# Moving the second ln_g multiplication, the quantisation of x and the squares within the issue orders of GpSimd, VectorE and ScalarE

## What is computed

```python
x = _layernorm(x + attn(x))                    # 16 heads of 32, every linear with a rank-16 update
x = _layernorm(x + x * scan(ctx * ctx))        # r = decay * r + ctx*ctx along the rows
x = _layernorm(x + ffn(x))

def ffn(x):
    h = silu(bitlinear158(x, w1, b1))          # 512 -> 2048
    h = gelu(h)
    h = layer_norm(h, ln_g, ln_b)              # (h - mean) * rsqrt(var + eps) * ln_g + ln_b
    return bitlinear158(h, w2, b2)             # 2048 -> 512
```

## Time and profile before

| what | value |
| --- | --- |
| median of three executions | 1051.56 us |
| the profiled execution, its own time | 1050.57 us |
| the profiled execution, its span | 1048.7 us |
| mean granted TensorE clock | 0.960 of full speed |
| busy: TensorE, VectorE, ScalarE, GpSimd | 945.9, 907.5, 827.6, 605.9 us |
| distance of one body from the next (565.94 to 623.98, starts of one multiplication by ln_g) | 58.0 us |

### The profile page before, as it was taken

How to read it: one execution, slowest core, us unless ns; L and a number is a source line. 1 busy time by engine, 2 the same in 40 slices (tenths; PEclk the granted TensorE clock), 3 DMA queues, 4 the chain that set the end, 5 groups by cost and what they waited for, 6 DMA issues and landing times.

```text
span 1048.7 us, 23313 instructions
## 1 busy us (share of the span) xinstructions
PE 945.9 (90%) x9260; PEld 650.5 (62%) x9260; DVE 907.5 (87%) x1490; ACT 827.6 (79%) x957; POOL 605.9 (58%) x767
## 2 busy tenths in 40 slices
PE   5998997999999999999999999999999999977515
PEld 3866756676677767676767766676767676644202
DVE  4678878999998999999999989999999999995766
ACT  3646686888979797988879897979888888977684
POOL 2332337474756759485756658494857576572643
PEclk9998998999999999999999999999999999988668
DMA  9432200223122121323131221323131321112213
GB/s 360 154 119 104 73 2 21 74 52 84 22 75 61 48 68 52 84 52 84 48 88 21 60 69 39 83 52 84 52 84 23 93 41 54 44 49 64 52 33 89
DMA packets 106352, 73.67 MB, mean 70 GB/s; under 512 B 91386, under 2 KB 91386, under 8 KB 104451
## 3 DMA queue, kind: packets, MB, share of 16 engines
q1 hardware_dynamic: 105522, 70.34, 24.4%
q10 hardware_dynamic: 720, 1.84, 0.5%
HBM read 41.73 MB, written 8.40 MB: 48 GB/s over the span
## 4 chain that ended last, share of the span: by engine, by line
DVE 34%; PE 28%; ACT 15%; issue 9%; POOL 7%; DMA 7%; SPq 1%; DVEq 0%; ACTq 0%; POOLq 0%
PE bank L1484 11%; PE bank L1345 7%; DVE neg_max L964 6%; DVE h L1095 6%; POOL h L549 5%; DMA xqT<-xq 5%; DVE stats L1021 3%; ACT h L725 3%; ACT junk L735 3%; ACT h L740 3%; PE bank L1485 3%; DVE fz L1100 2%; DVE qk_parts L987 2%; DVE rows L1037 2%; ACT L725 2%
## 5 line engine op out<-in xcount | busy, mean ns | idle before, releaser
L964 DVE TENSOR_REDUCE neg_max<-wave 128x8 f32<-128x2048 f32 x64 | 146.1, 2283 | 19.2 <-PE wave L1370 19.1
L549 POOL TENSOR_TENSOR h<-h,g_tile 128x2048 f32<-128x2048 f32 x30 | 139.4, 4645 | 39.1 <-ACT h L740 39.1
L657 ACT ACTIVATE probs<-wave 128x1024 f32<-128x1024 f32 x128 | 124.4, 1024 | 35.9 <-PE wave L1394 35.7
L1484 PE MATMUL bank<-w,xqT 128*128 128x512 fp8e4 x496 | 130.1, 386 | 23.7 <-DMA xqT<-xq 23.7
L439 POOL TENSOR_SCALAR attn_hi<-attn 128x256 fp32r<-128x256 f32 x64 | 30.2, 473 | 148.6 <-DVE attn L1003 132.9
L695 ACT ACTIVATE rows<-rows,rstd 128x512 f32<-128x512 f32 x96 | 74.3, 807 | 41.7 <-POOL rstd L455 23.8
L719 ACT ACTIVATE h<-bank,qx 128x512 f32<-128x512 f32 x124 | 83.9, 689 | 25.4 <-PE bank L1485 23.2
L1095 DVE TENSOR_TENSOR h<-h,b_tile 128x2048 f32<-128x2048 f32 x32 | 83.9, 2623 | 18.2 <-POOL h L549 18.1
L1484 PEld LDWEIGHTS bank<-w,xqT 128*128 128x128 bf16 x496 | 47.8, 99 | 81.4 <-issue 20.8
L1491 PE MATMUL bank<-w,hqT 128*128 128x512 fp8e4 x416 | 94.3, 380 | 0.2 <-DMA hqT<-h 0.2
L498 POOL TENSOR_TENSOR rows<-rows,bo_tile 128x512 f32<-128x512 f32 x32 | 51.6, 1633 | 71.1 <-DMA rows<-x 71.1
(11 more groups left out here) (184 smaller groups left out, 2841.9 us busy)
## 6 DMA issues: line engine op xcount, KB each, us to landing
ctx_sb<-ctxT SPq DMA_DIRECT2D x16, 512.0 KB, 3.7
rows<-x SPq DMA_DIRECT2D x16, 512.0 KB, 4.0
out<-rows SPq DMA_DIRECT2D x32, 256.0 KB, 2.5
xT_in<-xT SPq DMA_DIRECT2D x15, 512.0 KB, 4.7
h<-w1T SPq DMA_DIRECT2D x4, 1024.0 KB, 14.8
h<-w2T SPq DMA_DIRECT2D x4, 1024.0 KB, 4.9
h<-Wq SPq DMA_DIRECT2D x1, 1024.0 KB, 6.1
h<-Wk SPq DMA_DIRECT2D x1, 1024.0 KB, 9.7
```

Of the source, the lines that this page charges most:

```text
L549: po.tensor_tensor(h_of(b, q)[:, :], h_of(b, q)[:, :], g_tile[:, :], ALU.mult).then_inc(done, 1)
L657: ac.activation(probs[:, kt, :, :], wave[:, :, kt * T:(kt + 1) * T], ACT.Exp, scale=SM_SCALE).then_inc(S["probs_ready"], 1)
L964: dv.tensor_reduce(neg_max[:, :, :], wave[:, :, :].rearrange("p j (t k) -> p j t k", t=NT), axis=AX_X, op=ALU.max, negate=True).then_inc(S ...
L1484: pe.matmul(p[:, :], xqT[:, q, kc, :], w1[:, kc, n * FW:(n + 1) * FW], start=(kc == 0), stop=False)
```

## The change

Three issue orders change. On GpSimd the second half's multiplication by ln_g goes from before `inverse_std2` and `x_rms` to behind them. On ScalarE the squares of the first half go behind the second normalisation, and those of the second half from before `xq_store` to directly before `zq_store`. On VectorE the quantisation of x goes ahead of the second half's addition of ln_b. No instruction is added or removed, and the lead-in, the drain, SP's order and TensorE's order stay as they are.

```diff
@@ GpSimd, body(j)
                 if alive(j, 0):
                     attn_split(j, 1)
-                if alive(j, 2):
-                    g_mul(j - 2, 1)
                 if alive(j, 1):
                     inverse_std2(j - 1)
                     x_rms(j - 1)
+                if alive(j, 2):
+                    g_mul(j - 2, 1)
                 if alive(j, 3):
                     inverse_std3(j - 3, 1)
@@ ScalarE, body(j)
-                if alive(j, 2):
-                    z_square(j - 2, 0)
                 if alive(j, 1):
                     normalise(2, j - 1, 0)
                     normalise(2, j - 1, 1)
+                if alive(j, 2):
+                    z_square(j - 2, 0)
                 if alive(j, 0):
                     shiftT(j, 3)
                 if alive(j, -1):
                     v_store(j + 1, 0)
                 if alive(j, 0):
                     probs_of(j, 3)
-                if alive(j, 2):
-                    z_square(j - 2, 1)
                 if alive(j, 1):
                     xq_store(j - 1)
...
                 if alive(j, 0):
                     ctx_square(j)
                 if alive(j, 2):
+                    z_square(j - 2, 1)
                     zq_store(j - 2, 0)
@@ VectorE, body(j)
                 if alive(j, 0):
                     attn_norm(j, 2)
-                if alive(j, 2):
-                    z_add(j - 2, 1)
                 if alive(j, 1):
                     quantise_x(j - 1)
                 if alive(j, 2):
+                    z_add(j - 2, 1)
                     quantise_z(j - 2, 0)
```

## The result

The change makes the kernel slower: 1106.01 us in the median of four executions (1103.93 to 1109.27) against 1052.07 for the kernel before, run beside it. The ratio is 1.0515, with a 95% interval from 1.0486 to 1.0544. The prediction was 1105.

A forecast was written before the change was run, and what follows sets the result against it. VectorE's order was taken to bound the loop body, through x to TensorE and z to ScalarE. Nine bodies at 4.6 us, three at 3.4 and 2 us for body 15 made 53.6 us, so 1105 us; whole range 1089 to 1114.

The forecast's parts named there:

- What moves on GpSimd: GpSimd's ln_g multiplication starts 0.4 to 0.5 us ahead of VectorE's shift split; ScalarE's second normalisation some 2 us sooner.
- The hold: VectorE's split of the shift, L971, waits for GpSimd's multiplication to end, so VectorE loses 4.04 us.
- What comes back: On VectorE, L1066 in x's quantisation gives back 0.28 us, so the rounding of z ends 3.76 us later.
- z's path: ScalarE's SiLU 0 empties its PSUM bank late, so the fourth feed-forward product on TensorE starts 3.4 us late.
- TensorE's path: TensorE's transposes of the shift start 3.86 us late; absorbing the 0.78 us wait for x leaves 3.1.
- The clock: TensorE's new hole lowers its clock in nine of twelve bodies, costing 1.5 us where it falls, 4.6 us in all.
- The ends: Body 15, outside the twelve bodies, loses 2 us, between 0 and 3.8; body 2 loses nothing.
- Rival 1: The hold on VectorE comes without a fall of TensorE's clock: 43 us lost, 1094.5 us; chance 0.25.
- Rival 3: VectorE's L971 gets in first; the multiplication holds x's quantisation for 1.2 us instead: 4 us lost, 1056; chance 0.07.
- Rival 2: The multiplication never holds VectorE; x lands sooner and the gain, capped by SiLU 0, is 5 us, 1046; chance 0.06.

The follow-up runs named there:

- experiment 3: The changed kernel with the second half's ln_g multiplication one step further back on GpSimd, behind inverse_std3 of the second half: 1067.91 us.
- experiment 6: The changed kernel with the second ln_g multiplication of the bodies cut into four pieces of 512 columns: 1069.22 us.
- 7: The changed kernel with the second ln_g multiplication of the bodies replaced by one memset, so its result differs: 1045.19 us.
- experiment 5: The changed kernel with the first half of v's projection computed twice more on TensorE in bodies 3 to 14, filling its hole: 1091.03 us.
- experiment 4: The kernel before with only x's quantisation moved ahead on VectorE and the second half's squares moved on ScalarE: 1044.05 us.
- experiment 1: The kernel before with only GpSimd's second-half ln_g multiplication moved behind inverse_std2 and x_rms: 1110.8 us.

## Why the prediction was right

- **What moves on GpSimd.** x_rms was to end 3.91 us after the statistics, with the multiplication 3.9 to 4.0 us after them. It started after 3.87 (609.50 to 613.37), 0.53 us ahead of the split where I gave 0.4 to 0.5. ScalarE's second normalisation started 2.42 us after the statistics instead of 4.40, the 2 us sooner that I gave.
- **The hold.** 4.04 us were lost by the sum, and 3.87 were measured (4.04 less 0.17). The multiplication takes 4.54 us here, not 4.64, and starts a little sooner. The Trainium skill's statement in "SBUF — State Buffer", section "Who interferes with whom", that issue order decides and that two SBUF inputs on VectorE meet a read on GpSimd, agrees with experiments 3 (0.17 us when VectorE is first), 6 (one piece each) and 7 (0.17 us beside a memset).
- **What comes back.** The 0.60 us of L1066 fell to 0.17: 0.43, where I had given 0.28. The rounding of z ended 19.72 us after the statistics (609.50 to 629.22) instead of 16.31, 3.41 us later and not 3.76.
- **z's path, 3.4 us a body.** With the clock out of the way (experiment 5) the body is 3.29 us longer, and the fourth part of the feed-forward 3.13 later after the statistics.
- **TensorE's path.** The transposes of the shift were to be 3.86 us late; 8.71 us after the statistics instead of 5.06 is 3.65. Less the 0.78 that is absorbed that leaves 2.9, below the 3.13 of z's path in experiment 5, so without the clock TensorE doesn't decide; with it, it does, as the chain of waits of body 9 shows.
- **The clock.** The hole of 3.44 to 3.81 us was about as long as forecast, and the clock fell behind it. But two numbers were off, in opposite directions. I had it fall in nine of twelve bodies, for a total of 4.6 us each, without a row that gives the count. It fell in all twelve. In nine the body gained 4.2 us on average, in three 5.2. Nine at 4.6 and three at 3.4 are 51.6 us, and the measured sum is 53.6. That a count too low and a price too high came out so near is luck.
- **The ends.** 2 us were given to body 15 and the drain. They took 0.8, and what lies ahead of the twelve bodies, which has nothing to do with the change, another 0.9. So the 1 us between 1105 and 1106 says less than the body times do.
- **The rivals.** Rival 1, the hold without the clock, stood at 1094.5, and experiment 5 put it at 1091. Rival 3, VectorE first, stood at 1056, and experiment 3 gave 1068: the place was right and the price was too low by 1 us a body, mostly because it counted one held instruction of three. Rival 2 capped a gain by x at 1046, and experiment 4, which is that gain without the GpSimd move, gave 1044.

What stays open is why nearly equal holes came with 3.4 us of the lower clock in nine bodies and 6.8 in three, and which instructions with one input tensor are held and which not. Neither was tried.

## What to carry to other kernels

Before moving a long GpSimd instruction that reads SBUF, list what VectorE issues in the stretch where it will land, and look for instructions with two SBUF inputs: even the smallest of them waits until the GpSimd instruction ends, and everything behind it on VectorE waits too. Look at tensor_scalar instructions as well, as L1066 of the kernel before and L1071 and L1073 of experiment 3 were held with one input tensor. Half a microsecond in who starts first was worth 38 us here, so the distances of both engines from a common event (here the statistics) must be worked out before the move, and cutting the long instruction bounds the damage. A hold on one engine is paid a second time if it opens a hole on TensorE that brings the lower clock; the part that gains (x first) is best tried apart from the part that opens it.

## What the runs showed that I had not expected

- Idle stretches of TensorE of 3.4 to 3.8 us, once in each body between stretches of full work, brought the 1.2 GHz level every time, in 12 of 12 bodies of the changed kernel and 12 of 12 of experiment 1. Idles of 1.2 to 1.6 us in the bodies of experiment 6 didn't. Filling the long ones with repeated matmuls kept 2.4 GHz from 200 to 960 us and saved 15 us, although each of the twelve bodies had 2.8 us more TensorE work.
- The wait of a tiny VectorE instruction is booked as its own busy time: VectorE's busy total rose by 45.1 us with no instruction added, and no idle time of VectorE shows it.
- The second half's multiplication took 4.53 to 4.54 us in the twelve bodies of the changed kernel, 4.61 to 4.63 in experiment 5, and 4.62 to 4.66 before. Between the changed kernel and experiment 5 VectorE stands held beside it in the same way, and what differs is that TensorE idles or works. Why that would matter to GpSimd no run shows.
